# Moving a pair of VectorE blocks ahead of the output add, and copying the output accumulator through ScalarE

## The reference

```python
xn  = layernorm(x)                              # x: 16 x 2048 x 1024
# attention, 16 heads of 64
phi = lambda z: where(z > 0, z + 1, exp(z))
q, k, v = phi(xn @ Wq.T + bq), phi(xn @ Wk.T + bk), xn @ Wv.T + bv
kv    = einsum('bhnd,bhnm->bhdm', k, v)          # over the whole sequence
att   = einsum('bhnd,bhdm->bhnm', q, kv) / max(q . k.sum(n), 1e-6)
att   = att @ Wo.T + bo
# feed-forward: 8 trees of depth 7, 255 nodes each
L     = xn @ W_in.T + b_in                       # width 2040
path  = one-hot of the nodes met when each node sends left or right by L > 0
ffn   = (silu(L) * path) @ W_out.T
y     = x + att + ffn
```

## Time and profile before

| | us |
|---|---|
| median of 3 runs | 1383.93 |
| lowest, highest of them | 1379.01, 1411.93 |
| the profiled execution, device time | 1379.78 |
| its span on the slowest core (core 3) | 1378.7 |
| spans of the eight cores | 1372.2 to 1378.7 |

### The profile page before, as it was taken

How to read it: one execution, slowest core, us unless ns; L and a number is a source line. 1 busy time by engine, 2 the same in 40 slices (tenths; PEclk the granted TensorE clock), 3 DMA queues, 4 the chain that set the end, 5 groups by cost and what they waited for, 6 DMA issues and landing times.

```text
span 1378.7 us, 17563 instructions; the slowest of 8 cores (1372.2 to 1378.7 us)
## 1 busy us (share of the span) xinstructions
PE 1183.7 (86%) x6602; PEld 558.8 (41%) x6602; DVE 706.5 (51%) x1230; ACT 472.7 (34%) x592; POOL 8.5 (1%) x15
## 2 busy tenths in 40 slices
PE   2788989889779999998899989998999898988996
PEld 0334434344334444444344444444444444434443
DVE  3455556555544454455544554555445545555453
ACT  1454555555323322222233222222333222223331
POOL 1000000000000000000000000000000000000000
PEclk9999899899978999999988999998889999998898
DMA  9990110111260000100000001100000011000000
GB/s 174 195 182 31 62 61 32 62 34 60 39 99 31 31 31 31 62 31 32 31 31 31 31 31 57 35 32 31 31 31 31 31 48 44 31 31 31 31 16 31
DMA packets 21602, 68.28 MB, mean 50 GB/s; under 512 B 2071, under 2 KB 2071, under 8 KB 21520
## 3 DMA queue, kind: packets, MB, share of 16 engines
q1 hardware_dynamic: 14112, 50.40, 11.0%
q0 software_dynamic: 7408, 16.76, 7.8%
HBM read 67.13 MB, written 16.78 MB: 61 GB/s over the span
## 4 chain that ended last, share of the span: by engine, by line
PE 53%; DVE 24%; DMA 12%; issue 6%; ACT 4%; DVEq 1%; SPq 1%; POOL 0%; ACTq 0%; POOLq 0%
PE p_acc L750 16%; DMA s_x<-x 9%; PE p_acc L721 5%; PE p_acc L723 5%; PE p_tr L705 4%; PE p_kq L370 3%; DVE s_scr L540 3%; DVE s_qp L560 3%; DVE s_norm L544 3%; PE p_kq L376 3%; DVE s_phiq L535 3%; DVE s_acts L513 3%; DMA s_wkv<-wvt 3%; PE p_kq L346 3%; PE p_v L370 2%
## 5 line engine op out<-in xcount | busy, mean ns | idle before, releaser
L479 PE MATMUL p_L<-s_win,s_xnt 128*128 128x510 bf16 x1024 | 234.1, 381 | 12.3 <-DVE s_acts L513 11.6
L750 PE MATMUL p_acc<-s_wkv,s_mT 128*128 128x512 bf16 (+1 forms) x1024 | 226.5, 379 | 0.0
L492 ACT ACTIVATE s_acts<-p_L 128x1020 bf16<-128x1020 f32 x64 | 64.7, 1011 | 314.3 <-PE p_L L484 314.3
L479 PEld LDWEIGHTS p_L<-s_win,s_xnt 128*128 128x128 bf16 x1024 | 98.0, 98 | 142.8 <-issue 29.4
L750 PEld LDWEIGHTS p_acc<-s_wkv,s_mT 128*128 128x128 bf16 (+1 forms) x1024 | 98.8, 98 | 114.0
L502 DVE TENSOR_SCALAR s_dn<-s_acts 128x1020 bf16<-128x1020 bf16 x32 | 13.7, 427 | 208.2 <-ACT s_acts L492 208.2
L721 PE MATMUL p_acc<-s_wo,s_ap 128*128 128x512 bf16 x256 | 120.2, 469 | 0.0
L723 PE MATMUL p_acc<-s_wo,s_ap 128*128 128x512 bf16 x256 | 116.6, 455 | 0.0
L460 PE MATMUL p_acc<-s_wq,s_xnt 128*128 128x512 bf16 x256 | 98.7, 386 | 3.0 <-ACT s_xnt L273 3.0
L201 DVE TENSOR_SCALAR s_xn<-s_x,s_stats 128x1024 bf16<-128x1024 f32 x32 | 25.9, 813 | 144.2 <-DMA s_x<-x 144.2
L671 ACT COPY s_qpt<-p_tr 128x512 bf16<-128x512 bf16 x32 | 18.7, 585 | 233.0 <-PE p_tr L661 233.0
(11 more groups left out here) (119 smaller groups left out, 1540.4 us busy)
## 6 DMA issues: line engine op xcount, KB each, us to landing
s_x<-x SPq DMA_DIRECT2D x64, 512.0 KB, 4.2
y<-s_out SPq DMA_DIRECT2D x32, 512.0 KB, 2.9
s_win<-wint POOLq DMA_DIRECT2D x1, 4080.0 KB, 92.8
s_wkv<-woutt POOLq DMA_DIRECT2D x1, 3840.0 KB, 28.7
s_wkv<-wkt POOLq DMA_DIRECT2D x1, 2048.0 KB, 22.8
s_wkv<-wvt POOLq DMA_DIRECT2D x1, 2048.0 KB, 37.1
s_wq<-wqt POOLq DMA_DIRECT2D x1, 2048.0 KB, 48.6
s_wo<-wot POOLq DMA_DIRECT2D x1, 2048.0 KB, 64.2
```

What stands on the lines that cost most here:

```text
L479: T.matmul(p_L[:, 512 * k4:512 * k4 + 510], lhs, s_win[:, WIDTH * c + 510 * kk:WIDTH * c + 510 * (kk + 1)], start=(c == 0), stop=False)
L492: i = S.activation(s_acts[pb][:, 1020 * phase:1020 * (phase + 1)].rearrange("p (b c) -> p b c", b=2), srcL, AF.Tanh, scale=0.5)
L750: i = T.matmul(acc[:, 512 * half:512 * (half + 1)], lhs, s_wkv[0:kj, 1024 * j + 512 * half: 1024 * j + 512 * (half + 1)], start=False, sto ...
```

## The change

Three edits, all in the second loop. (1) `emit_phiq_pair(t+1)` is emitted right after `emit_mask_levels(t+1)`, ahead of the transposes of tile t+2, W_out, the output adds, the load of x and the second half of the logits, where before it was the last thing of the turn. (2) The two halves of `p_acc[t%2]` are copied by ScalarE into a new SBUF tile `s_wtmp` (128x1024 f32), and VectorE adds `s_x` to that copy rather than to PSUM. (3) `p_acc[t%2]` counts as free after the second ScalarE copy rather than after the adds. The arithmetic is the same.

```diff
+    s_wtmp = al("s_wtmp", [128, D], F32).ap()
@@ after mask levels of t+1
             nxt["mlev"] = emit_mask_levels(t + 1, av[1:])
+            nxt.update(emit_phiq_pair(t + 1, nxt["ev_e2"], nxt["ev_qb"]))
@@ output of tile t
-        em.wait("V", ev_oh[0], ev_prev_out[buf])
-        i = V.tensor_tensor(s_out[buf][:, 0:512], acc[:, 0:512],
+        em.wait("S", ev_oh[0], war_scr.get("wtmp"))
+        i = S.copy(s_wtmp[:, 0:512], acc[:, 0:512])
+        ev_c0 = em.sig(i, "ss")
+        em.wait("S", ev_oh[1])
+        i = S.copy(s_wtmp[:, 512:1024], acc[:, 512:1024])
+        ev_c1 = em.sig(i, "ss")
+        war_acc[t % 2] = [ev_c1]
+        em.wait("V", ev_c0, ev_prev_out[buf])
+        i = V.tensor_tensor(s_out[buf][:, 0:512], s_wtmp[:, 0:512],
                             s_x[t % 4][:, 0:512], ALU.add)
         ev_f0 = em.sig(i, "sv")
-        em.wait("V", ev_oh[1])
-        i = V.tensor_tensor(s_out[buf][:, 512:1024], acc[:, 512:1024],
+        em.wait("V", ev_c1)
+        i = V.tensor_tensor(s_out[buf][:, 512:1024], s_wtmp[:, 512:1024],
                             s_x[t % 4][:, 512:1024], ALU.add)
         ev_fin = em.sig(i, "sv")
-        war_acc[t % 2] = [ev_f0, ev_fin]
+        war_scr["wtmp"] = ev_fin
@@ end of the turn
-            nxt.update(emit_phiq_pair(t + 1, nxt["ev_e2"], nxt["ev_qb"]))
```

## The result

The changed kernel takes 1476.6 us (median of 8 runs, 1474.6 to 1477.4) against 1380.1 us before in the same comparison (median of 8): the ratio is 1.0696, 95% interval 1.0683 to 1.0709. It is slower by 7.0%; 1485 us was forecast. In some runs the cores of one die are granted a lower clock and the run is some per cent longer; all ratios, and the times given for the experiments, are taken without such runs, which leaves e10 a single one. The profiled execution has a span of 1474.4 us on its slowest core (core 0; 1467.8 to 1474.4 on the eight), 95.7 us more than before.

The account below looks back on a forecast made before the run. PE sets the pace but waits in a loop through VectorE, SP's load of x and ScalarE. Steps sum to 32.8 us, 34.6 with half clock, against 30.73; 29 turns and end corrections give +105 us, 1485 us, range 1440 to 1520.

Parts of the forecast that it names:

- 4 the pair: VectorE's L535 to L560, moved directly behind the mask levels: 7.14 us on the chain, covered only by the rest of W_out.
- 5 adds: Two output adds back to back on VectorE: 0.79 us between starts and 0.77 us to SP's store.
- 6 store, load of x: From SP's store and load of x, behind the second add, to L201 on VectorE: 4.89 us.
- 8 logits, with half clock: The 18 logits matmuls on PE behind L513: 4.08 us at full clock, plus 1.8 us for half clock.
- 9 to the next transposes: From L661 to the next mask transposes L705, with `s_qp` ready: 2.2 us.
- clock term: Half clock on the logits after PE's 7.1 us wait: 3.6 us of it, costing 1.8 us per turn.
- rival with a held clock: The clock does not fall at PE's wait before the logits: turn 32.8 us, time 1433 us, chance 0.10.
- rival with a longer half clock: Half clock lasts 6.7 us or reaches into L661 to L705: turn 36.1 us, time 1530 us, chance 0.08.
- x is there in time: At step 6 the load does not wait behind the late add, saving 4.9 us per turn: 1321 us, chance 0.05.
- needed, not a gain: Freeing `p_acc` by the copy: needed because the q matmuls of t+2 start 15.9 us after L705, before the adds end.
- copies without cover: ScalarE copies ahead of the adds: free in a steady turn, 0.7 us per turn if VectorE's later arrival did not cover them.
- price that the prediction quotes for a transfer: The skill's 2.0 us plus bytes at 436 GB/s: 512 KB load 3.2 us alone, 4.4 us behind an equal store.

Follow-up runs that it names:

- e10: Changed kernel with second-half activations ahead of the adds and x loaded early, but adds from PSUM and no ScalarE copies: 1429.8 us, one run, no ratio.
- e9: Changed kernel with the load of x put ahead of the store of y in SP's queue, both still behind the second add: 1490.3 us, ratio 1.0744.
- e4: Changed kernel with 110 unused transposes per turn filling PE's wait ahead of the logits: 1431.8 us, ratio 1.0373 to the kernel before.
- e5: Changed kernel, copies included, but `p_acc` counts as free only after the second output add: 1431.8 us, ratio 1.0377 to the kernel before.
- e2: Kernel before with only the ScalarE copies of the output block, pair left at the end of the turn: 1381.4 us, ratio 1.0012.
- e1: Kernel before with only the pair moved, VectorE still adding from PSUM without ScalarE copies: 1428.1 us, ratio 1.0353.
- e3: Changed kernel with the load of x issued ahead of W_out, in front of the store of y: 1283.9 us, ratio 0.9297 to the kernel before.
- e7: Changed kernel with second logits half, its tanh and activations ahead of the output adds, x still late: 1315.4 us, ratio 0.9514 to the kernel before.

## Why the prediction was right, point by point

The direction, the mechanism and the size held: 1485 us forecast, 1476.6 measured. The chain of the turn, by the prediction's steps, against the turn shown above:

| step | forecast, us | measured, us | from, to |
|---|---|---|---|
| 1 mask transposes to copy | 1.2 | 1.16 | 928.92, 930.08 |
| 2 ScalarE to L503 | 5.15 | 5.15 | 930.08, 935.23 |
| 3 masks | 4.51 | 4.51 | 935.23, 939.74 |
| 4 the pair | 7.14 | 7.14 | 905.87, 913.01 |
| 5 adds | 1.56 | 1.36 | 913.01, 914.37 |
| 6 store, load of x | 4.89 | 4.59 | 914.37, 918.96 |
| 7 L202, L514 | 2.09 | 2.08 | 918.96, 921.04 |
| 8 logits, with half clock | 5.9 | 5.83 | 921.04, 926.87 |
| 9 to the next transposes | 2.2 | 2.05 | 926.87, 928.92 |
| sum | 34.6 | 33.87 | mean of 29 turns 34.19 |

The excess of the forecast over the measured turn lies mostly in steps 5, 6 and 9 (0.65 us together in this turn, 0.4 in the mean). Step 5 took 0.79 us from L535 to L540, where the second reads what the first wrote; two adds that don't depend on each other start 0.60 us apart. The clock term came out right, 3.6 us of half clock assumed and 3.4 us measured on the logits, but in part by luck: it was picked by likeness from three lengths, and the prediction did not work out when the clock falls. In the turn shown it is at half for some 6.5 us, as long as the 6.7 us at 902 that the prediction set aside, and only because it falls some 3 us before the wait ends do 3.4 us of it lie on the logits. In e9 it falls so that more of it lies there. Turns 29 and 30 took 26.7 and 22.1 us, where 28 and 22.1 were taken.

The wait at L666 went, L480 waits 198.9 us in 31 times (some 200 were forecast; 6.4 us each), and L202 still waits 4.8 us each. The mean clock of the cores, forecast at or a little below 0.90, is 0.900 to 0.907. The rival with a held clock fell with e4: the clock does fall, and where it is kept by force the kernel takes 1432 us, which is what that rival gave (1433). The rival with a longer half clock needed 6.7 us of it behind the wait, where 3.4 us were measured. The rival "x is there in time" was rightly placed and priced too high: with x early the kernel took 1283.9 us, not 1321. The clock then holds too, where about 1 us per turn had been allowed for it, which is 29 of the 37 us. This rival didn't come about by itself since the change leaves the store and load behind the adds, as was argued.

One part of the working was wrong although the total came out. The prediction costed the release of `p_acc` by the copy as "needed, not a gain", and the copies at nothing because VectorE comes late to the adds. The first was wrong, and e5 shows it: without the early release the changed kernel is some 44 us faster. PE would have waited in two places and run its half clock on the q matmuls, in the shadow of the wait for x. The sum was not hurt by this, because it followed the actual order and put the half clock on step 8. The prediction also said that the copies without cover would cost 0.7 us per turn; e2 shows the 0.7 us in the timeline and none of it in the time, because the clock gives it back. The price that the prediction quotes for a transfer is from a fit for transfers that GpSimd issues, and SP issues these; the sum did not use it.

Open is what decides when the clock falls: why it falls later in e2 than in the kernel before behind a wait of the same 3.01 us, and why in e9 the shorter wait is followed by more half clock. Both would need the clock to be moved by itself.

## What to carry to other kernels

When work is moved ahead in a strictly ordered queue, list everything it is moved past, DMA issues included, and walk the whole loop once: here a pair that was late for one consumer was put in front of three that were later still. Find the transfer that waits for nothing but its place in a queue first; with x early the same change turned from a loss of 7% to a gain of 2%. And when PE must wait somewhere in a turn, let it wait as early as it can, with work behind the wait that nobody is waiting for: the half clock that follows is then free. This holds only while something later is waited for anyway, as in e1 and e5. In e10 nothing was, and the wait ahead of the q matmuls was paid in full, half clock included.

## What the runs showed of the hardware

- The length of a wait doesn't decide alone whether the clock falls. PE waited 1.80 us before the logits in e3 and ran on at full clock; in e7 waits of 0.60 and 1.23 us, with short 64-wide matmuls between them, were followed by half clock. Waits of the same 3.01 us at the transposes of `s_qp` left the clock at half before they ended in the kernel before, and at full for another 1.2 us in e2.
- The fall can come after PE has started again: in e1 the first four q matmuls from 924.49 on ran at full clock, after a wait of 3.51 us, and then the rate halved. The Trainium skill ("TensorE: Matmul & The Clock Gate", Part 1) has activity lift the clock and idleness lower it; these rows agree in that the fall follows an idle stretch and the rise follows matmuls.
- Idle-time filling pays: 110 useless transposes per turn made the kernel some 45 us faster (e4).
- A f32 copy of 128x512 out of PSUM costs ScalarE 0.586 us, the same as the cast to bf16 in the earlier trace rows, and VectorE's f32 add costs 0.69 us from PSUM and from SBUF alike.
